# A fused macaron layer on eight cores: where the copies of the transposes, the recurrence's output and one quantization stand in a slot

## The reference, cut to what matters

```
x = x + 0.5 * ffn(layernorm(x))      # both ffn with the same weights
x = x + gated_recurrence(layernorm(x))
x = x + 0.5 * ffn(layernorm(x))

ffn(x)  = bitlinear(gelu(bitlinear(x, w1, b1)), w2, b2)       # 1024 -> 4096 -> 1024
bitlinear(x, w, b) = act_quant(rmsnorm(x)) @ weight_quant(w).T + b
act_quant(x): s = 127 / max|x| of the row;  round(x * s) / s
weight_quant(w): ternary, one scale for the matrix

gated_recurrence(x): r = sigmoid(x Wa + ba); i = sigmoid(x Wx + bx)
    a = exp(-8 softplus(-Lam) r);  b = sqrt(1 - a*a) * i * x
    h[t] = a[t] * h[t-1] + b[t]       # scan over the 4096 positions
```

## Time and profile before

| | us |
|---|---|
| median of 3 runs | 4954.83 |
| lowest and highest of them | 4643.77, 5005.6 |
| the profiled execution, its own time | 4643.38 |
| its span on the slowest core (core 2) | 4641.8 |
| spans of the eight cores | 4631.0 to 4641.8 |

### The profile page before, as it was taken

The page is one execution under the profiler, slowest core; times in us unless marked ns, Lnnn a source line. Parts: engine busy times, 40 slices in busy tenths (PEclk is TensorE's granted clock), DMA queues, the critical chain, the costliest instruction groups (busy, mean ns, idle before and its releaser), DMA issues.

```text
span 4641.8 us, 75615 instructions; the slowest of 8 cores (4631.0 to 4641.8 us)
## 1 busy us (share of the span) xinstructions
PE 4225.2 (91%) x23463; PEld 2242.4 (48%) x23463; DVE 3528.0 (76%) x4614; ACT 2790.7 (60%) x3464; POOL 972.4 (21%) x1541
## 2 busy tenths in 40 slices
PE   1699999999999989999999999999999999999999
PEld 0344455555555545454545445555555555444444
DVE  4888777777777777777777777777777777777786
ACT  4555666666666666666666666666666666555553
POOL 0122222222222222222221212222122221222221
PEclk9999999999999999999999999999999999999999
DMA  9455655556555555565555565555556555455555
GB/s 287 153 168 161 203 186 177 182 186 198 184 187 186 177 182 182 188 193 191 186 177 180 181 193 183 197 186 181 177 182 197 185 195 177 147 186 172 167 188 181
DMA packets 366185, 857.59 MB, mean 185 GB/s; under 512 B 39368, under 2 KB 45664, under 8 KB 365664
## 3 DMA queue, kind: packets, MB, share of 16 engines
q1 hardware_dynamic: 365792, 852.76, 56.5%
HBM read 740.41 MB, written 112.20 MB: 184 GB/s over the span
## 4 chain that ended last, share of the span: by engine, by line
PE 70%; DVE 16%; issue 7%; ACT 3%; DMA 2%; SPq 1%; DVEq 0%; POOL 0%; ACTq 0%; POOLq 0%
PE f_pm L486 29%; PE f_po L642 27%; PE aux L874 9%; DVE f_h L499 3%; PE aux L463 2%; DVE w2T L932 2%; DVE w2T L923 2%; ACT f_A L470 2%; DMA p_ring<-L_ffn_w 2%; PE aux L946 1%; DVE f_col L510 1%; PE aux L850 1%; DVE f_q L540 1%; SPq L62 1%; DVE f_col L435 1%
## 5 line engine op out<-in xcount | busy, mean ns | idle before, releaser
L486 PE MATMUL f_pm<-w1T,f_q1T 128*128 128x512 fp8e4 x8192 | 1837.6, 380 | 13.7 <-DVE f_h L499 4.7
L486 PEld LDWEIGHTS f_pm<-w1T,f_q1T 128*128 128x128 f16 x8192 | 795.0, 98 | 924.7 <-issue 24.1
L642 PE MATMUL f_po<-w_x,f_A 128*128 128x512 fp8e4 x4960 | 1161.9, 389 | 3.9 <-DMA w_x<-w2x 2.2
L505 ACT ACTIVATE f_h<-f_h 128x1024 f32<-128x1024 f32 x512 | 539.5, 1057 | 865.0 <-DVE f_h L499 859.6
L499 DVE SCALAR_TENSOR_TENSOR f_h<-f_pm,f_col,f_b1c 128x1024 f32<-128x1024 f32 x512 | 654.8, 1279 | 222.2 <-PE f_pm L486 217.1
L669 DVE SCALAR_TENSOR_TENSOR f_xb<-f_po,f_col,f_xb 128x512 f32<-128x512 f32 x496 | 370.1, 748 | 583.7 <-PE f_po L642 557.4
L642 PEld LDWEIGHTS f_po<-w_x,f_A 128*128 128x128 f16 x4960 | 498.2, 101 | 569.6 <-issue 60.4
L510 DVE TENSOR_REDUCE f_col<-f_h 128x1 f32<-128x1024 f32 x512 | 621.5, 1214 | 29.1 <-ACT f_h L505 17.1
L874 PE MATMUL aux<-w2T,g_w 128*128 128x256 bf16 x4096 | 536.0, 290 | 110.9 <-ACT f_A L470 110.9
L517 ACT ACTIVATE f_sqj<-f_h 128x1024 bf16<-128x1024 f32 x512 | 540.4, 1056 | 26.0
L874 PEld LDWEIGHTS aux<-w2T,g_w 128*128 128x128 bf16 x4096 | 418.6, 103 | 214.3 <-issue 119.2
(11 more groups left out here) (102 smaller groups left out, 3855.0 us busy)
## 6 DMA issues: line engine op xcount, KB each, us to landing
w_x<-w2x SPq DMA_DIRECT2D x1736, 256.0 KB, 5.3
g_w<-wg SPq DMA_DIRECT2D x256, 512.0 KB, 5.7
p_ring<-L_ffn_w SPq DMA_DIRECT2D x64, 512.0 KB, 16.4
f_xb<-L_attn_x SPq DMA_DIRECT2D x64, 512.0 KB, 6.1
xs<-f_xb SPq DMA_DIRECT2D x64, 512.0 KB, 6.4
g_xg<-xs SPq DMA_DIRECT2D x32, 1024.0 KB, 8.1
xs<-g_xg SPq DMA_DIRECT2D x32, 1024.0 KB, 5.2
f_xb<-xs SPq DMA_DIRECT2D x64, 512.0 KB, 5.6
```

Source lines behind the costliest of these rows:

```text
L486: a = put("tensor", lambda t, k=k, hf=hf, o=o: t.matmul(pm[i][:, hf * 512:(hf + 1) * 512], q1T[:, k * 128:(k + 1) * 128], w1T[:, o:o + 512 ...
L505: tj["gelu%d" % p] = put("scalar", lambda s: s.activation(hg[:, sl], hg[:, sl], AF.Gelu), waits=[ev])
L642: a = put("tensor", lambda t, k=k, c=c, w=w: t.matmul(po[:, bank * 512:(bank + 1) * 512], lhs[:, k * 128:(k + 1) * 128], w[:, c * 512:(c + ...
```

## The change

Three things are done. The first half's `t2` is put into the queues ahead of `evict1(cur, 1)`, and the second half's ahead of `evict1(cur, 2)`. On TensorE the order stays as it is (transposes behind `mm1(cur, 1)` and behind `mm1(cur, 2)`), and VectorE has no part in `t2`; so what changes is ScalarE's order: the copy of the first half now stands before gelu 1, and that of the second before gelu 2. Second, `recur(j, -1)` stands directly behind `evict1(cur, 3)`, ahead of `gmax(cur, 2)`, `gmax(cur, 3)` and `scale2`. These are VectorE's operations alone, so only VectorE's order changes, and only in stage 0, where `recur(j, -1)` has a VectorE operation, the add L954 of `g_tr_out`. Third, in the 32 slots of stage 0 with a live group, two of the four quantizations ran on ScalarE (L536); now all four run on VectorE (L540).

```
--- before.py
+++ after.py
@@ -1121,10 +1121,11 @@
                             centre(nxt)
                         if cur is not None:
                             mm1(cur, 1)
+                        if pre is not None:
+                            t2(pre, order[0])
+                        if cur is not None:
                             evict1(cur, 1)
                         recur(j, -4)
-                        if pre is not None:
-                            t2(pre, order[0])
                         if nxt is not None:
                             quant1(nxt)
                         recur(j, -3)
@@ -1133,20 +1134,21 @@
                         if cur is not None:
                             gmax(cur, 0)
                             mm1(cur, 2)
+                        if pre is not None:
+                            t2(pre, order[1])
+                        if cur is not None:
                             evict1(cur, 2)
                         if odd:
                             product_out(K, 3)
                         if cur is not None:
                             gmax(cur, 1)
-                        if pre is not None:
-                            t2(pre, order[1])
-                        if cur is not None:
                             mm1(cur, 3)
                             evict1(cur, 3)
+                        recur(j, -1)
+                        if cur is not None:
                             gmax(cur, 2)
                             gmax(cur, 3)
                             scale2(cur)
-                        recur(j, -1)
                         if not drain:
                             row(j, 0)
                             row_out(j, 0)
@@ -1155,9 +1157,8 @@
                             t1(nxt)
                         recur(j, 0)
                         if cur is not None:
-                            act = R0 <= j < R0 + 3 * NG and (j - R0) % 3 == 0
-                            for i, p in enumerate((0, 1, 2, 3) if j % 2 == 0 else (2, 3, 0, 1)):
-                                quant2(cur, p, act and i >= 2)
+                            for p in ((0, 1, 2, 3) if j % 2 == 0 else (2, 3, 0, 1)):
+                                quant2(cur, p)
                             square(cur, 0)
                             square(cur, 1)
                         if even:
```

## The result

The changed kernel is faster: the ratio of its time to that of the kernel before is 0.9499, 95% interval 0.9458 to 0.954. The profiled execution took 4413.98 us, with spans of 4399.8 to 4412.4 us on the eight cores; the four executions shown range from 4408.55 to 5052.24 us, with a median of 4621.1, beside 4799.43 for four executions of the kernel before (4643.77 to 5005.6). Two of the four executions of either kernel are 7 to 15% longer than its fastest (in the changed kernel the cores of one half of the chip are then at a mean clock of 0.83 or 0.88 instead of 0.99); the medians mix both kinds, and the ratio compares only the others. So the forecast of 4424 us for an execution like the profiled one is 0.2% off, and the median lies 121 us above the range's end of 4500.

A forecast was written before the change was run, and what follows sets the result against it. TensorE, busy 91% of the span, was taken as the bound, its waits as the gain. Stage-2 and stage-0 terms summed to 13.7 us in each of 16 repetitions, 219 us: 4643.4 to 4424 us, range 4360 to 4500.

The forecast's parts named there:

- the sum: Slots of stages 2 and 0: 5.7 + 4.1 + 0.3 + 3.6 = 13.7 us per repetition, 219 us in 16.
- Copies: Stage 2: copies ahead of gelu end the gates' waits, returning 5.7 us in even and 4.1 in odd slots.
- What is late behind the copies: Even stage-2 slot: `t1` and the next gate wait for tanh, about 0.6 and 0.5 us.
- The add, and L841: Stage 0: earlier add returns 0.3 us (even), 3.6 (odd); new waits for L841 of 3.8 and 1.3 us.
- The clock: Slow TensorE work behind new stage-0 waits: 1.9 us behind the 3.8 us wait, none behind the 1.3.
- Quantizations: Stage 0: two more quantizations on VectorE, 1.3 us per slot, lengthen both waits for L841 by that much.
- (a): Rival: VectorE gives nothing back in stage 0, only stage 2 pays: 157 us, 4487; chance 0.19 with what lies between.
- (b): Rival: even stage-0 wait leaves the clock alone, VectorE makes up 1 to 2 us: 4362 to 4378; chance 0.17.
- (c): Rival: copies do not free stage 2's gates, only stage 0 pays: 62 us, 4581; chance 0.08 including gains too small.
- (d): Rival: later gelus delay VectorE's maxima in all 128 slots, up to 450 us lost against 219: 4874; chance 0.04.
- The upper end of the sum: Whole kernel: 4451 us if the 1.3 us wait also brings slow matmuls, 16 x 1.7 = 27 us.

The follow-up runs named there:

- copies_only: The kernel before with only both halves' `t2` copies moved, ahead of gelu 1 and gelu 2; 4480 us, ratio 0.9646.
- split kernel: The changed kernel with two of the four quantizations back on ScalarE in stage 0; 4368.39 us, ratio 0.9408.
- sums_late: The changed kernel with the two sums of even stage-0 slots put behind the recurrence's part at 1, so behind L841; 4348 us, ratio 0.9364.
- first_copy: The kernel before with only the first half's copy moved ahead of gelu 1; ratio 1.0019.
- add_only: The kernel before with only `recur(j, -1)` moved ahead of the last two maxima; 4509.1 us, ratio 0.9707.

## Why the prediction was right, and where it was wrong

**What the range was about.** The time given as a median, 4621.1 us, is outside 4360 to 4500. The step that failed is the first term of the sum: "I sum against the profiled execution, 4643.4 us. That is the lowest of the three runs shown, 311 us under their median." Figure and range were thus for executions like the lowest, though two of the three times before stood 311 and 362 us higher, and the sum puts such executions at nothing. The runs showed that they come in the changed kernel too: two of its four times stand at 4828 and 5052. The median of four executions before is 4799.43 us, 156 above the term used; with it the sum would have given 4580, 41 under the median measured. What makes an execution long stays open. The mechanism has no part in this miss.

**Copies.** The two stage-2 slots gained 4.3 and 5.7 us where 4.1 and 5.7 were walked, and `copies_only` was forecast at 4484 and measured at 4480. The step moves both copies; only the second does anything.

**What is late behind the copies.** The estimate was 0.6 us for `t1` and 0.5 for the next gate; measured are 8.9 / 16 = 0.56 and 5.6 / 16 = 0.35.

**The add, and L841.** The walk gave 1.3 and 3.8 us for the two waits for L841; measured are 1.15 and 3.61. The total of 82 us is 74.8. The slots of stage 0 are 33.1 and 34.0 us, as walked.

**The clock.** The new 3.61 us wait costs 8.76 - 7.07 = 1.69 us behind it, against 1.9 taken from before; the 1.15 us wait costs nothing. That is the sum's choice, not its bounds. Over all 16 even slots it is 27 us on this core, as two of the waits cost nothing and three cost 2.7. The mean granted clock is 0.991 to 0.994 where about 0.98 was expected; the sum itself, which takes away 6.2 of 8.1 us of slow work, would have led from 0.963 to 0.99. With these, one repetition lost 14.1 us for the 13.7 of the sum, which is 6 of the 10 us between 4424 and 4414.

**Quantizations.** "Straight on the new path", 1.3 us each: the split kernel returned 42 us by the ratios, where 38 were expected. The step said that both waits would be 1.3 us shorter; they are, as 2.3 and nothing.

**Rivals.** (a) would have left stage 0 without gain; it gained 3.6 and, less the slow stretch, 0.5 us. `sums_late` shows that VectorE still had room. (b) came true in 2 of 16 even slots only, where the wait left nothing slow behind it, and VectorE made up 0.2 us, not 1 to 2. (c) falls with `copies_only`. (d) falls with `first_copy` and `copies_only`: L510 waits less for gelu after the change (0.6 us) than before (17.1), and as little with the second copy alone (0.4), which gelu 3 no longer has ahead of it.

**Slips without effect.** The list of waits before was not only start-up beyond the three named: 12.4 us before L946 for L932 lie in the recurrence, 16 times 0.8, and stay (12.0). The upper end of the sum is 4451 in one place and 4455 in another. The DMA shares of the earlier trace rows go from 0.53 to 0.66, not from 0.50 to 0.58. VectorE's busy time rose by 28 us, not 43, though L540 alone took 42 more.

## What to carry to other kernels

When an engine at the head of the list of waits is released by another engine's operation, look at what stands ahead of that operation in its own queue and whether it was ready earlier: here one copy behind one gelu and one add behind two maxima were 5.9% of the time (the ratio 0.9408), with no work removed. Then walk the releasing engine's queue on to its next product, because work that is free before such a move can lie on the path after it: the same edit of two quantizations measured 0.0% in one order and 0.9% in the other. And decide, before giving a time, which of the executions shown it is for.

## What the runs showed of the hardware

A wait's price beyond its own length does not follow from its length alone. In the odd slots of stage 2 of the kernel before, the waits of 2.2 to 2.45 us before a gate were followed by slow matmuls in all 16 repetitions (3.55 us for 16 of them). In `add_only`, in the same slots, waits just as long were followed by full speed in 6 of the 16 (TensorE's timeline):

```profile
2014.28 1.91 PE L874 MATMUL aux<-w2T,g_w 128*128 128x256 bf16 x16 [2.45 <-ACT f_A L470]
2016.02 3.62 PE L642 MATMUL f_po<-w_x,f_A 128*128 128x512 fp8e4 x16
```

The same holds for two of the 16 waits of 3.6 us in the changed kernel (four on cores 0 and 3), this one among them:

```profile
3058.35 1.06 PE L850 MATMUL aux<-ident_f,g_xn 128*128 128x128 f32 x8 [3.60 <-DVE g_xn L841]
3059.25 7.07 PE L486 MATMUL f_pm<-w1T,f_q1T 128*128 128x512 fp8e4 x32
```

In the traces read here no wait of 1.6 us or less was followed by slow work, and every one of 4.3 us and more was. Between them the runs show either. What decides it was not tried. It means that an edit can bring more or less than its waits, by where the rest of the schedule puts the waits that remain: here the two moves together saved 24 us of slow work less than the two one by one.
